# Storing the queries' first parts at ScalarE's copy, moving POOL's memory sets, and packing the first group's keys from ScalarE's queue

## What is computed

```python
h = concatenate([patches(x) @ W_tok, txt], axis=1)            # 16 x 324 x 192
h = h + L0_attn(layernorm(h))   # softmax over tokens, circular convolution with the values (here by a DFT)
h = h + L0_ffn(layernorm(h))    # 192 -> 768 -> 192 with GELU
h = h + L1_attn(layernorm(h))   # 12 heads of 16; 196 shared tokens are added to keys and values
h = h + L1_ffn(layernorm(h))    # router picks 162 tokens for each of 4 experts;
                                # a second attention over the 324 tokens, and an MLP
```

## Time and profile before

| | us |
|---|---|
| median of 3 runs | 2008.18 |
| lowest and highest | 1998.37, 2015.78 |
| the profiled execution | 2008.32 |
| its span | 2006.6 |

### The profile page before, as it was taken

The page is one execution under the profiler, slowest core; times in us unless marked ns, Lnnn a source line. Parts: engine busy times, 40 slices in busy tenths (PEclk is TensorE's granted clock), DMA queues, the critical chain, the costliest instruction groups (busy, mean ns, idle before and its releaser), DMA issues. The chain is left out here.

```text
span 2006.6 us, 41460 instructions
## 1 busy us (share of the span) xinstructions
PE 1840.8 (92%) x11904; PEld 1246.2 (62%) x11904; DVE 1259.3 (63%) x3509; ACT 1073.4 (53%) x2549; POOL 290.7 (14%) x441
## 2 busy tenths in 40 slices
PE   4789999999999999999999997778999999999996
PEld 3566676676676676666666664355666666666664
DVE  4266676676775766776776765345767656565663
ACT  1245455555555455555555553435666566665663
POOL 4301111111111111120120111010001000010000
PEclk9899999999999999999999998789999999999998
DMA  4302212212212212222221222123333433334331
GB/s 152 77 18 66 65 45 66 64 45 65 64 45 65 64 48 63 65 61 52 65 68 49 60 64 71 51 74 77 97 95 94 101 101 93 97 96 113 81 96 30
DMA packets 161304, 143.62 MB, mean 72 GB/s; under 512 B 32284, under 2 KB 136488, under 8 KB 161064
## 3 DMA queue, kind: packets, MB, share of 16 engines
q1 hardware_dynamic: 157448, 136.69, 25.4%
q0 software_dynamic: 2304, 4.79, 0.9%
q10 hardware_dynamic: 1440, 0.75, 0.1%
HBM read 82.79 MB, written 50.16 MB: 66 GB/s over the span
## 5 line engine op out<-in xcount | busy, mean ns | idle before, releaser
L956 ACT ACTIVATE prob<-sps 108x324 f32<-108x324 f32 x1536 | 626.4, 441 | 465.5 <-PE sps L1368 448.2
L1226 DVE TENSOR_REDUCE mxh<-mps 108x1 f32<-108x324 f32 x1152 | 520.0, 487 | 274.1 <-PE mps L1402 269.9
L1368 PE MATMUL sps<-qpack,kpack 128*108 128x324 bf16 x1536 | 434.1, 318 | 20.2 <-ACT prob L956 10.7
L1402 PE MATMUL mps<-kpack,qpack 96*108 96x324 bf16 x1728 | 384.6, 296 | 44.8 <-DMA kpack<-scr_k 27.8
L1368 PEld LDWEIGHTS sps<-qpack,kpack 128*108 128x108 bf16 x1536 | 185.1, 128 | 212.0 <-ACT prob L956 118.4
L1402 PEld LDWEIGHTS mps<-kpack,qpack 96*108 96x108 bf16 x1728 | 211.8, 130 | 161.9 <-issue 56.0
L1383 PE MATMUL aps<-prob,v 128*32 128x324 f32 x3072 | 299.7, 454 | 4.3 <-issue 1.0
L1226 DVE TENSOR_REDUCE mxs<-mps 108x2 f32<-108x392 f32 x288 | 161.1, 559 | 84.9 <-PE mps L1402 83.4
L1354 PE MATMUL lin<-yT,w 128*128 128x324 f32 x576 | 184.2, 451 | 13.1 <-ACT g L856 11.1
L773 POOL CAST piece<-rest 128x324 bf16<-128x324 f32 x96 | 44.3, 461 | 745.2 <-DVE rest L1057 740.7
L1354 PEld LDWEIGHTS lin<-yT,w 128*128 128x128 f32 x576 | 102.6, 192 | 59.3 <-issue 28.6
(11 more groups left out here) (150 smaller groups left out, 2326.5 us busy)
## 6 DMA issues: line engine op xcount, KB each, us to landing
qpack<-scr_q SPq DMA_DIRECT2D x96, 243.0 KB, 3.2
kpack<-scr_k SPq DMA_DIRECT2D x96, 121.5 KB, 3.3
scr_q<-piece SPq DMA_DIRECT2D x32, 243.0 KB, 3.0
scr_k<-piece SPq DMA_DIRECT2D x32, 243.0 KB, 3.5
kpack<-scr_k SPq DMA_DIRECT2D x96, 81.0 KB, 3.1
bc<-rec_d SPq DMA_DIRECT2D x112, 60.8 KB, 2.4
scr_q<-piece SPq DMA_DIRECT2D x32, 162.0 KB, 3.3
scr_q<-piece SPq DMA_DIRECT2D x64, 81.0 KB, 3.0
```

Of the source, the lines that this page charges most:

```text
L956: nc.scalar.activation(prob[0:rows, n % NP, :], sps[0:rows, n % 2, 0:N], ACT.Exp, scale=SCALE).then_inc(att.exped.sem, 1)
L1226: nc.vector.tensor_reduce(dst, src, AX.X, ALU.max, negate=True).then_inc(att.mps.free["dve"].sem, 1)
L1368: mm(sps[0:rows, n % 2, 0:N], kpack[:, 4 * q + n % 4, k * att.rows:k * att.rows + rows], qpack[:, 4 * q + n % 4, :], start=True, stop=True ...
L1402: done = mm(bank[0:P, s * SC:s * SC + k1 - k0], qpack[0:6 * D, 4 * q + hd, t * P:(t + 1) * P], kpack[0:6 * D, 4 * q + hd, k0:k1], start=Tr ...
```

## The change

There are three edits. (1) `to_dram` stores the slots of `scr_q` that hold the first parts as soon as ACT's copies of blocks 0 and 1 are there (signal `first`), and the others after POOL's `third`. There are eight DMAs as before. (2) POOL's memory sets `REST` wait for `ln1_done` of sample 0. (3) In the attention `one`, the three DMAs that pack group 0's keys are issued from ACT's queue by a new function `first_keys` instead of SP's; it waits for `scr_in` and for the sums of group 0 of the sample before. The word pack0 is moved from slot 12 into slot 11, between val_1 and the first "m". SP still packs group 0's queries. The second edit is one line.

```diff
-    "s zv s val_0.0 val_0.1 zs p s val_1 m s m s zt m m m s dft_0.0 m p s m dft_0.1 m m s m dft_1.0 m m m s dft_1.1 m a",
-    "of pack0 s s a m s s m",
+    "s zv s val_0.0 val_0.1 zs p s val_1 pack0 m s m s zt m m m s dft_0.0 m p s m dft_0.1 m m s m dft_1.0 m m m s dft_1.1 m a",
+    "of s s a m s s m",
...
+                def queries(m, p1, r, n):
+                    sp.dma_start(scr_q[r:r + n, 128 * m:128 * m + p1, :].rearrange("s p n -> p s n"),
+                                 piece[0:p1, m, Q_PARTS[r]:Q_PARTS[r] + 1, :].broadcast_to([p1, n, N])).then_inc(att.scr_in.sem, 16)
...
+                for m, p1 in ((0, 128), (1, 64)):
+                    sp.wait_ge(att.first.sem, att.first.at(j, m + 1))
+                    queries(m, p1, 0, 3)
                 for m, p1 in ((0, 128), (1, 64)):
                     sp.wait_ge(att.third.sem, att.third.at(j, m + 1))
-                    for r, n in ((0, 3), (3, 2), (5, 1)):
...
+                    queries(m, p1, 3, 2)
+                    queries(m, p1, 5, 1)
+                keys(1, 64, 0, 64)
+                sp.wait_ge(att.third.sem, att.third.at(j, 3))
+                keys(2, 0, 64, C)
...
+                if att is one and q == 0:
+                    return
...
                             pool.wait_ge(root_known[0].sem, root_known[0].at(j, 1))
+                            pool.wait_ge(ln1_done.sem, ln1_done.at(j, 1))
                             memsets(REST, len(FEW))
...
+            def first_keys(j):
+
+                act.wait_ge(one.scr_in.sem, one.scr_in.at(j, 128))
+                act.wait_ge(one.summed.sem, one.summed.at(j - 1, 4 * one.kt))
+                for r, n in ((0, 3), (3, 2), (5, 1)):
+                    act.dma_start(kpack[r * D:(r + n) * D, 0:4, 0:N],
+                                  scr_k[0:n].rearrange("s (d h) n -> (s d) h n", d=D)[:, 0:4, :]).then_inc(one.pack_in[0].sem, 16)
...
+                if name == "pack" and k == 0:
+                    first_keys(j)
+                    return
```

More of the change, by code:

```diff
@@ L593, in to_dram, with keys @@
                     sp.wait_ge(one.pack_in[-1].sem, one.pack_in[-1].at(B - 1, 64))
+                def queries(m, p1, r, n):
+                    sp.dma_start(scr_q[r:r + n, 128 * m:128 * m + p1, :].rearrange("s p n -> p s n"),
+                                 piece[0:p1, m, Q_PARTS[r]:Q_PARTS[r] + 1, :].broadcast_to([p1, n, N])).then_inc(att.scr_in.sem, 16)
+                def keys(m, p0, c0, c1):
+                    sp.dma_start(scr_k[:, c0:c1, :].rearrange("s p n -> p s n"),
+                                 piece[p0:128, m, :, :]).then_inc(att.scr_in.sem, 16)
+                for m, p1 in ((0, 128), (1, 64)):
+                    sp.wait_ge(att.first.sem, att.first.at(j, m + 1))
+                    queries(m, p1, 0, 3)
                 for m, p1 in ((0, 128), (1, 64)):
                     sp.wait_ge(att.third.sem, att.third.at(j, m + 1))
-                    for r, n in ((0, 3), (3, 2), (5, 1)):
[L597 to L602, removed]
+                    queries(m, p1, 3, 2)
[3 more added lines that the diff above has]
+                keys(2, 0, 64, C)
             def pack(att, j, q):
```

## The result

| | before | after |
|---|---|---|
| median, us | 2008.81 (4 runs) | 2052.66 (4 runs, 2050.1 to 2061.46) |
| the profiled execution | 2008.32 | 2061.46 |
| its span | 2006.6 | 2059.8 |

The ratio of the times is 1.023, with a 95% interval of 1.0176 to 1.0285: the kernel became 44 us slower.

The account below looks back on a forecast made before the run. PE, busy 92% of the span, was taken as the bound, with its waits for group 0's keys. 2008.3 + 38.0 (waits) + 3.9 (iteration -1) + 14.9 (clock) - 6.9 (start) = 2058.2 us; range 2036 to 2086.

Parts of the forecast that it names:

- Two of the signs: At the first "m", PE waits 4 us or more in iterations 0 to 13, with a total near 70 us.
- ACT's place behind val_1: On ACT's in-order queue, group 0's key loads cannot issue before val_1 ends: 686.75 where SP's issue was 683.68.
- The wait's length: PE's wait at group 0's first "m" grows from 1.59 to 4.3 us in 14 iterations: +38.0 us.
- iteration -1: PE's wait for group 0's keys grows from 0.44 to 4.3 us there: +3.9 us.
- The clock: PE's clock falls behind each of 14 waits, against five now, at 1.65 us a fall: +14.9 us.
- rival (c): PE's clock falls in each wait and stays low for long: 52 in place of 14.9, 2095 us; chance 9%.
- Edit 1 behind edit 3 is worth nothing: Earlier stores complete scr_in 0.8 us sooner, but the key loads then wait for ACT: 0.
- Edit 2: At the start, later memory sets free DVE's three instructions, and zt starts at 24.5, not 31.36: -6.9 us.
- rival (d): At the start, the copy at L1126 is held up by the memory set: +6, 2064 us; 68% with the forecast.
- Rival (a): Between val_1's end and PE's "m", ACT's loads land no later than SP's did: 1976 us; chance 5%.
- Iteration 14: No val_1 there; ACT reaches pack0 near 1203.1, where SP's issue lay as well: 0.

Follow-up runs that it names:

- SP late from its own queue: Against the changed kernel, group 0's three key loads go out from SP again, after ACT's copy of val_1: 2060.62 us, ratio 1.0266.
- the filled kernel: Against the changed kernel, PE makes four useless products between val_1 and the wait for group 0's keys: 2023.0 us, ratio 1.0084.
- edit 2 alone: Against the kernel before, only POOL's memory sets wait for the first layer norm: 2003.11 us, ratio 0.9969.
- group 1 held back: Against the changed kernel, pack0 stands before zv and SP's group 1 loads wait until group 0's keys have landed: 1976.2 us, ratio 0.9848.
- an earlier issue alone: Against the changed kernel, pack0 stands before zv on ACT, with group 1's loads not held back: 2021.97 us, ratio 1.0078.

## Why the prediction was right, and where its terms were off

The time (2052.66 us, forecast 2058.2) and the mechanism were right. Two terms were off in opposite directions, and that they balanced is luck. Two of the signs that it named did not hold either: no wait of iterations 0 to 13 reached 4 us (3.04 to 3.35), and the total was 55.4 us and not near 70.

- **ACT's place behind val_1: right.** The loads begin 0.17 us after val_1's end (716.90 against 716.73; the forecast had 0.15). SP late from its own queue gave the same waits.
- **The wait's length: mis-sized.** 4.3 us forecast, 3.2 us measured (44.7 / 14). Most of the error was the landing: 3.1 us, the median over all such loads, was used, and 2.2 was measured for the last one. The reason given, "queues are calm then", spoke for a value near the lower end, 2.1, which stood in the same row. The issue took 0.43 us and not 0.55. The term became +22.4 and not +38.0; iteration -1 gave +3.2 and not +3.9.
- **The clock: mis-sized the other way.** One fall of 1.65 us was set for each wait. The number of falls was right, all 14. But in 11 of them the clock was low for some 6 us behind the landing and not for 3.4, and cost 2.7 us (7.44 - 4.76). The row that told it was there: behind the wait of 4.31 us the 6 us had 0.50 throughout. The price came from short waits, which were the wrong rows for a long one. Against the forecast of +14.9 the profile gives +33 at half of the time at the lower clock (iteration -1 with it), or +27 by the filled kernel's 0.4; the upper end of +40 holds both. Against rival (c) it was said that dense work brought the clock back within 4 us. That did not carry over: PE was busy throughout behind these landings too. In iteration 7 before, the clock came back 5.3 us after the landing; it was low for 3.4 us, and fell 1.9 us behind the landing.
- **Edit 1 behind edit 3 is worth nothing, alone about 0.8 us a wait.** The second half is right: 0.8 us a wait, and 19 us in all with the clock. The first is not measured by itself; the loads begin at val_1's end with and without edit 1, 0.17 us behind it in iteration 7.
- **Edit 2: right in size, one step untested.** 6.9 us forecast; 6.1 in the profile, 6.2 alone. The held `zexp` came as said. The copy at L1126 took 0.20 us, from 25.58 to 25.78, so rival (d) did not come about. But it was not put to the test: the second set of `kpack` began only at 26.20, behind the copy. Beside the copy ran the end of a short set (25.02 to 25.72), so whether a long set holds such a copy up stays open. The six instructions of "of" (the prediction counts five) took up to 0.55 us each, as long as before, and four of them ran at least in part beside sets. That the start moves to the first "m" as a whole was too simple, as edit 2 alone shows (4.9 of 6.7 us).
- **Rival (a): the forecast of its price was good, its mechanism too simple.** It said 1976 us if ACT's loads landed in time. That is what group 1 held back gave, but an earlier issue alone gave 2022. With the word behind val_1, as in the change, no run came near its condition, a landing within 1.6 us of val_1's end. The rival forgot that SP's queue, once rid of group 0's keys, starts group 1 sooner.
- **Iteration 14: right to say no change.** Its wait is 4.70 us (4.31 before), ACT's loads start at 1257.55, 0.18 us behind the end of PE's last product, and group 1's went out of SP 0.75 us before them. With group 1 held back this wait was 2.35 us.

## What to carry to other kernels

A DMA that is moved to a compute engine's queue goes out when that engine gets to it: compare the moment of the old issue with the end of the last instruction ahead of the new place, and if the consumer finishes that same instruction, the transfer's whole latency is exposed. Splitting one queue in two also drops the order between urgent and later loads; write it out with a wait. And price a PE wait with the clock behind it, from a row whose wait is as long as the one that is expected: here the clock cost about as much again as the wait.

## What the runs showed of the hardware

- **The lower clock lasted longer behind longer waits.** In iterations 0 to 13 of all runs, waits of up to 1.2 us had no fall behind them. Waits of 1.3 to 2.0 us were followed by no fall or by 3.4 us at 1.2 GHz, waits of 2.0 to 2.9 us by none, 3.4 or 6.4 to 6.8 us, and waits of 3.0 to 3.9 us by 3.4 us in a few cases and by 5.5 to 6.8 us in most. The time at the lower clock cost 0.4 to 0.5 of its length: 0.4 by the filled kernel, and 0.5 leaves a rest that agrees within 4.7 us in 936 over the kernels with such falls.
- **Useless work in a wait paid.** 2.34 us of products in each of 16 waits made the kernel 29 us faster, since the granted clock then stayed at 1.00 behind the waits of iterations 0 to 13.
- **Time to landing depends on what runs beside it.** In iteration 7 the same three loads took 2.2 to 2.4 us in the kernel after, with nothing else issued in the 2 us before, 2.8 to 3.2 us before the change, between other loads of one queue, 2.7 to 3.0 us half a us behind the queries' load alone, and 4.5 us when the 486 KB of group 1 went out of a second queue at the same time.
